# Weights loaded and split ahead of the first attention; experts chosen by the least 1+exp(-z); hot rows fetched at stage 3; the first maxima of layer F interleaved

## The chip, the cores and the metric

The kernel runs on one core of one Trainium2 chip. The time is the device time in microseconds (us) of one execution. Five engines work side by side, each on its own list of instructions, and wait for each other on semaphores: TensorE (PE, with its weight load as PEld), VectorE (DVE), ScalarE (ACT), GpSimd (POOL) and SyncE (SP), which issues most of the DMAs. TensorE runs at one of two clocks, 1.2 or 2.4 GHz; the profile gives the granted share (0.50 or 1.00).

## The reference, cut to what matters

Eight sequences (batches 0 to 7) of 512 tokens by 128 go through two layers.

```python
x = x + A(layernorm(x))      # A: z = layernorm(x); 16 heads of causal softmax(z_h k_h) v_h, k = z Wk + bk,
                             # then z + gelu(o + bv) @ Wf + bf
x = x + F(layernorm(x))      # F: 8 heads, 8 experts
# in F, per token and head:
gates = sigmoid(x @ w_gate)                 # 8 per head
sel = argmax(gates, axis=-1)
gm = one_hot(sel) * gates                   # only the chosen expert's gate is left
values = einsum(gm, value_experts, x)       # the values are those of the chosen expert, times its gate
out = softmax(q k / 8, causal) @ values
out = einsum(gm, output_experts, out)       # the chosen expert again, on the way out
```

All weights are the same for the eight batches.

## The kernel before

One batch after another goes through layer A's attention (`attention_a` on PE and DVE, `attention("A", b)` on ACT and POOL), the `turn` (gelu, projection back, layer norm of layer F), `experts` (gates, queries and keys, expert values) and layer F's attention, in which the work on batch b+1 (its normalised input, its keys, its first maxima) is already mixed. Every engine has its own program, written out by hand; the order in the code is the order on the engine, and a wait in it holds up all that is behind it on that engine.

**Precision.** Every weight and activation that PE multiplies is split in a high and a low half (`wq_h`, `wq_l`), so a projection is three matmuls (lines 426 to 428, `mm3`). The high half is a copy on ACT, the low half a subtraction on DVE. The weights of layer F (`wq`, `wkf`, `wg`: 0.5 MB; `ve`: 2 MB) are loaded by four DMAs at the end of the restacking of batch 0 (line 407), into space that `hots` and `oe_sb` use later, and split when ACT and DVE come to group 2 of batch 0's attention A (`expert_weights_high`, `expert_weights_low`, `SPLIT_AT`).

**Attention.** Heads go in 4 groups, each group in 3 stages (the causal triangle of 4 tiles of 128 keys: tile 0, tile 1, tiles 2 and 3). A *max unit* (PE scores into `ps_max`, DVE masks them and takes row minima, line 1096) and its *denominator* (ACT exp with sum, line 812) come first; 12 units a group in A, 6 in F. Then `negate` (DVE) forms the negative of maximum plus logarithm, PE transposes it, ACT copies it to `mt_a` or `mt_f`, and SP writes it by DMA as extra rows (`maxima_rows`, line 345, semaphore `mrow`) into the stacked queries, so that the second pass of scores (`ps_exp`) comes out normalised. ACT takes its exp (line 870), POOL cuts the triangle (line 992), PE weighs the values (line 589). Group g+2's max units are mixed into group g's scores; groups 0 and 1 need theirs ahead.

**Stacked operands.** Layer A's queries and keys are cut into three bf16 parts, written to DRAM (`parts_q`, `parts_k`, line 296) and read back in stacked rows (lines 303, 306, 314) into `s1q` and `s2k`, of which 96 rows are multiplied. Rows that carry nothing must hold zeros: before, DVE zeroes all of `s1q` (line 1334) and POOL all of `s2q` and `s2k` (lines 1006, 1007). Layer F's queries and keys go from `pt` to `s1q`, `s1k`, `s2q`, `s2k` by 12 DMAs for each pair of heads (`restack_f`, line 334, semaphores `pair_sent0` and `pair_sent1`), 48 for a batch; pairs 2 and 3 reuse the space of pairs 0 and 1 in `pt`.

**experts(f).** PE makes the gates (bank 4) and 8 projections `qk` (u = 0 to 7; even ones queries, odd ones keys). ACT copies the high half (line 919, `qk_hi`), DVE makes the low half (line 1269, `qk_lo`), and SP sends a pair as soon as its two low halves are there. After u = 3, 5 and 7 come 12, 10 and 10 of the 32 *expert values* (n = 0 to 31, token tile and expert): three matmuls into bank n % 4; the first expert of a tile is copied by ACT, the other seven are picked by DVE with a predicated copy (line 1296, 28 of them). The banks of `qk` before are u % 2. The picks need `hot`, the one-hot choice that `gate_ops` computes on DVE. Before, in 7 steps: g_w = 1 + exp(-z); its reciprocal (the gates, 256 columns, line 1219); their maximum over 8 experts; which equal it; times a rank, so that ties go to the first; the maximum of that; which equal it. `outputs_end(f-1)` (line 1156) adds the last batch's residual after u = 0, and SP stores it (line 373) in `store(b-1)`, which stands ahead of `restack_f` in SP's list. Layer F's first 12 max units are mixed into the values from n = 20 on, one for each n; ACT takes their denominators after all of `experts`, at the head of `attention("F", b)`.

**The way out.** `hots` (the chosen rows, 64 partitions by 8 KB twice, from `hot_d`) is fetched four times a batch by DMAs that ACT issues (line 791), at the stages in `HOTS_AT`; DVE multiplies with it (`choose`, line 1146) from unit 14 of layer F on.

## Time and profile before

| | us |
|---|---|
| median of 3 runs | 1428.21 |
| lowest and highest | 1423.2, 1431.45 |
| the profiled execution, whole | 1432.81 |
| its span, first to last instruction | 1430.8 |
| PE busy in the span | 1186.2 (83%) |
| DVE, ACT, POOL busy | 895.1, 903.9, 213.8 |
| mean granted TensorE clock | 0.934 |

The chain of work that ended last is spread over many lines; 14% of it is "issue", time in which an engine waited for nothing that the page names, the longest pieces of it 10.85 us at 52.58 us and 3 us at 99.21 us. Batches follow each other every 168 to 171 us. A timeline row gives start and length in us, engine, line, what is written and read, and in brackets the idle time of the engine before it and what ended it.

### The profile page before, as it was taken

The page shows a single profiled execution, that of the slowest core. Times are in us where ns is not written, and L with a number is a line of the kernel's source. Part 1 is how long each engine was busy: PE and PEld are TensorE (multiplying, and loading weights), DVE is VectorE, ACT ScalarE, POOL GpSimd, SP SyncE. Part 2 cuts the span into 40 slices and gives each one's busy share as a digit, 9 for nine tenths or more (in the row PEclk, how much of TensorE's full clock was granted, in tenths as well). Part 3 has the DMA queues.
Part 4 walks back from the last instruction along what each step waited for, and adds up shares of the span by engine and source line. Part 5 has one row for each costly group of instructions (what it writes and reads, how often), then busy time and mean ns, then how long its engine had stood idle before and what let it go on. Part 6 is the DMA issues. An engine that isn't in the chain of part 4 may idle for free.

```text
span 1430.8 us, 19696 instructions
## 1 busy us (share of the span) xinstructions
PE 1186.2 (83%) x5720; PEld 644.8 (45%) x5720; DVE 895.1 (63%) x2786; ACT 903.9 (63%) x2551; POOL 213.8 (15%) x264
## 2 busy tenths in 40 slices
PE   2567988888987889788897898878898789978888
PEld 1113753256532564236542474325653356424653
DVE  5552857648574676737676485755757477673855
ACT  1784387935778266962769447783677827696361
POOL 3011011201112011120111111120111211111010
PEclk9566999999999999999999999999999999999999
DMA  2401734126421453206432073313632155320723
GB/s 80 125 2 61 179 87 94 31 68 141 113 54 33 113 138 94 61 3 149 117 78 60 25 172 101 80 31 84 149 95 49 33 129 125 90 61 3 174 64 74
DMA packets 64177, 122.32 MB, mean 85 GB/s; under 512 B 14099, under 2 KB 29843, under 8 KB 59683
## 3 DMA queue, kind: packets, MB, share of 16 engines
q1 hardware_dynamic: 58950, 87.50, 24.5%
q10 hardware_dynamic: 5120, 33.56, 10.5%
q8 instruction: 46, 0.75, 0.2%
q14 instruction: 61, 0.50, 0.1%
HBM read 61.11 MB, written 9.06 MB: 49 GB/s over the span
## 4 chain that ended last, share of the span: by engine, by line
PE 42%; ACT 20%; DVE 19%; issue 14%; POOL 2%; DMA 1%; ACTq 0%; SPq 0%; DVEq 0%; POOLq 0%
ACT masked L812 9%; ACT pt L870 8%; PE ps_o L589 8%; PE ps_m L598 7%; DVE masked L1096 5%; PE ps_m L426 3%; PE ps_exp L506 3%; PE ps_exp L507 3%; PE ps_m L427 2%; PE ps_m L428 2%; PE ps_max L693 2%; PE ps_exp L508 2%; DVE val L1296 2%; PE ps_exp L426 2%; DVE at L1146 2%
## 5 line engine op out<-in xcount | busy, mean ns | idle before, releaser
L1096 DVE CUSTOM_DVE_ANT_0 masked<-ps_max,mask 128x512 f32<-128x512 f32 (+3 forms) x768 | 353.5, 487 | 210.5 <-PE ps_max L506 90.4
L812 ACT ACTIVATE masked<-masked,low 128x512 f32<-128x512 f32 (+3 forms) x768 | 427.0, 559 | 71.2 <-DVE low L1096 67.2
L870 ACT ACTIVATE pt<-ps_exp 128x384 f32<-128x384 f32 (+1 forms) x576 | 293.2, 523 | 125.7 <-PE ps_exp L508 69.9
L992 POOL TENSOR_SCALAR_AFFINE_SELECT pt<-pt 128x512 f32<-128x512 f32 (+2 forms) x192 | 137.1, 714 | 742.0 <-ACT pt L870 742.0
L598 PE MATMUL ps_m<-at,oe_sb 128*128 128x512 f32 x416 | 219.1, 616 | 5.7 <-DVE at L1146 3.5
L506 PE MATMUL ps_exp<-s1q,s2k 96*128 96x128 bf16 (+3 forms) x512 | 137.1, 325 | 96.5 <-ACT pt L870 83.0
L589 PE MATMUL ps_o<-pt,val 128*32 128x128 f32 (+6 forms) x1536 | 193.6, 481 | 9.1 <-POOL pt L992 9.1
L1146 DVE TENSOR_TENSOR at<-osb,hots 128x512 f32<-128x512 f32 x208 | 143.3, 690 | 32.2 <-PE ps_m L598 32.2
L506 PE MATMUL ps_max<-s2k,s1q 96*128 96x512 bf16 (+3 forms) x512 | 138.6, 320 | 20.1 <-DVE low L1096 11.9
L506 PEld LDWEIGHTS ps_exp<-s1q,s2k 96*128 96x128 bf16 x512 | 42.3, 100 | 248.3 <-ACT pt L870 197.6
L812 ACT ACTIVATION_READ_ACCUMULATOR masked<-masked,low 128x1 f32 x768 | 150.3, 196 | 0.0
L507 PE MATMUL ps_exp<-s1q,s1k 128*128 128x256 f32 (+2 forms) x256 | 100.8, 404 | 14.8 <-issue 11.6
L1296 DVE COPY_PREDICATED val<-osb,ps_exp 128x512 f32<-128x512 uint32 x128 | 92.0, 734 | 26.5 <-PE ps_exp L428 26.4
L589 PEld LDWEIGHTS ps_o<-pt,val 128*32 128x32 f32 (+1 forms) x1536 | 53.5, 122 | 90.2 <-issue 58.9
L506 PEld LDWEIGHTS ps_max<-s2k,s1q 96*128 96x128 bf16 x512 | 48.8, 100 | 95.1 <-DVE low L1096 46.4
L598 PEld LDWEIGHTS ps_m<-at,oe_sb 128*128 128x128 f32 x416 | 70.2, 192 | 39.0 <-DVE at L1146 27.6
L507 PE MATMUL ps_max<-s1k,s1q 128*128 128x256 f32 (+2 forms) x256 | 86.5, 347 | 1.3 <-DVE low L1096 1.3
L919 ACT ACTIVATE pt<-ps_m 128x512 fp32r<-128x512 f32 x64 | 38.3, 598 | 73.9 <-PE ps_m L428 72.3
L508 PE MATMUL ps_max<-s2k,s2q 96*128 96x256 f32 (+2 forms) x256 | 84.3, 339 | 0.0
L508 PE MATMUL ps_exp<-s2q,s2k 96*128 96x256 f32 (+2 forms) x256 | 84.0, 338 | 0.0
L1317 DVE TENSOR_TENSOR x<-ps_max,x 128x512 f32<-128x512 f32 x8 | 5.5, 692 | 124.4 <-PE ps_max L693 124.4
L507 PEld LDWEIGHTS ps_exp<-s1q,s1k 128*128 128x128 f32 x256 | 50.4, 197 | 69.3 <-issue 49.7
(156 smaller groups left out, 1750.1 us busy)
## 6 DMA issues: line engine op xcount, KB each, us to landing
hots<-hot_d ACTq DMA_DIRECT2D x64, 512.0 KB, 6.6
s1q<-pt SPq DMA_DIRECT2D x128, 128.0 KB, 2.3
s1k<-pt SPq DMA_DIRECT2D x128, 128.0 KB, 2.3
s1q<-parts_q SPq DMA_DIRECT2D x96, 96.0 KB
s2k<-parts_k SPq DMA_DIRECT2D x96, 96.0 KB
s2q<-pt SPq DMA_DIRECT2D x64, 128.0 KB, 2.3
s2k<-pt SPq DMA_DIRECT2D x64, 128.0 KB, 2.3
parts_q<-pt SPq DMA_DIRECT2D x24, 128.0 KB, 2.3
```

The costliest lines, as they stand in the source:

```text
L426: mm(dst, lh, rh, start=True, stop=False)
L506: return mm(dst, l1[0:KROWS, h, l2], r1[0:KROWS, h, r2], start=True, stop=True)
L507: mm(dst, l1[0][:, h, l2], r1[0][:, h, r2], start=True, stop=False)
L508: return mm(dst, l1[1][0:KROWS, h, l2], r1[1][0:KROWS, h, r2], start=False, stop=True)
L589: last = mm(ps_o[g % 2][j * w:j * w + w, qt * P:S], val[:, kt, h * w:h * w + w], pt[:, (n % 2) * 4 + j, c0:c1], start=kt == 0, stop=kt == 3)
L598: mm(ps_m[1][:], oe_sb[:, u], chosen_o(u), start=u == 0, stop=u == T * E - 1).then_inc(at_used.sem, 1)
L812: last = nc.scalar.activation(e, e, ACT.Exp, bias=low[:, g % 2, c:c + 1], scale=-1.0, accum_out=den[:, g % 2, c:c + 1])
L870: nc.scalar.activation(pt[:, (n % 2) * 4 + j, 0:c1 - c0], ps_exp[u % 2][:, c0:c1], ACT.Exp).then_inc(exp_done[k].sem, 1)
L992: nc.gpsimd.affine_select(out=v, in_=v, compare_op=ALU.is_ge, fill=0.0, base=0, pattern=[[0, HG[k]], [0, m], [1, P]], channel_multiplier=- ...
L1096: last = v.tensor_tensor_reduce(out=masked[:, u % JUNK, c0:c0 + w], in0=src[:, c0:c0 + w], in1=mask[:, S - w:S], scale=-1.0, scalar=POS, o ...
L1146: v.tensor_tensor(chosen_o(u), osb[:, u // E], hots[:, u // E % 2, u % E], ALU.mult).then_inc(at_done.sem, 1)
L1296: v.copy_predicated(val[:, t].rearrange("p (h k) -> p h k", k=64), pick, ps_m[BANK[("F", "moe1", n)]][:].rearrange("p (h k) -> p h k", k=6 ...
```

## The change

Five edits are made.

1. **Start, SP.** The four loads of layer F's weights stand behind the five loads of `x`, `ident`, `wk`, `wv`, `bk`, ahead of the constants. The memsets of `s1q`, `s2q`, `s2k` on DVE and POOL are gone; in their place three DMAs fill rows 64 to 95 of each with zeros (32 partitions by 16 KB each), behind a wait for the constants in DRAM. The rows of ones and the parts of k come behind a wait for these zeros.
2. **Start, ACT and DVE.** The weights are split ahead of attention A of batch 0, ACT's half behind `k_part1(0)`, DVE's behind `values_a(0)`.
3. **experts, DVE and PE.** The choice is made on g_w = 1 + exp(-z) itself: the minimum over the experts, which are at most that, rank, maximum, which equal. The reciprocal is taken of the 32 minima alone. The first two steps stand ahead of u = 0, the others between u = 0 and u = 2; `log_gates` follows u = 2 and `outputs_end(f-1)` u = 3. `qk` uses banks u % 4.
4. **experts, the first max units of layer F.** They stand at n = 13, 14, 16, 17, 19, 20, 22, 23, 25, 26, 28, 29, on PE, DVE and ACT alike: ACT takes the denominators there, no longer behind the loop. `negate` of group 0 moves from n = 27 to 23, its transpose from 30 to 25, and ACT copies `mt_f` at 27.
5. **HOTS_AT.** In layer F the first fetch of `hots` moves from stage 1 to stage 3 (of 12).

```diff
-BANK.update({("F", "qk", u): u % 2 for u in range(8)})
+BANK.update({("F", "qk", u): u % 4 for u in range(8)})
...
-MAX_FROM, NEGATE_AT, TRANSPOSE_AT = 20, 27, 30
+NEGATE_AT, TRANSPOSE_AT, COPY_AT = 23, 25, 27
+MAX_AT = {13 + 3 * m // 2: (m,) for m in range(N_MAX)}
...
-HOTS_AT = {("F", 1): 0, ("F", 9): 1, ("A", 0): 2, ("A", 4): 3}
+HOTS_AT = {("F", 3): 0, ("F", 9): 1, ("A", 0): 2, ("A", 4): 3}
...
+            for dst, src in ((raw["wq"], wq), (raw["wkf"], wkf), (raw["wg"], wg),
+                             (ve_raw, ve.rearrange("p (e n) -> p e n", n=S))):
+                sp.dma_start(dst, src).then_inc(w_in[2].sem, 16)
             sp.dma_start(zeros_d, consts[5:9]).then_inc(cst.sem, 16)
...
-            sp.wait_ge(cst.sem, cst.count(0, 16 * 3))
-            sp.wait_ge(set_p.sem, set_p.count(0, 3))
...
+            sp.wait_ge(cst.sem, cst.count(0, 16 * 3))
+            for dst in (s1q, s2q, s2k):
+                sp.dma_start(dst[64:96].bitcast(F32).rearrange("p h n -> p (h n)"), zeros_d[0].partition_broadcast(32)
+                             ).then_inc(zero_rows.sem, 16)
...
             parts_to_dram(0, "q")
+            sp.wait_ge(zero_rows.sem, zero_rows.count(0, 16 * 3))
+            sp.dma_start(ks[STACK:STACK + PARTS], onesb_d.rearrange("p (h n) -> p h n", n=S)).then_inc(cst.sem, 16)
             parts_to_dram(0, "k")
...
-            for dst, src in ((raw["wq"], wq), (raw["wkf"], wkf), (raw["wg"], wg),
-                             (ve_raw, ve.rearrange("p (e n) -> p e n", n=S))):
-                sp.dma_start(dst, src).then_inc(w_in[2].sem, 16)
...
-                    if g == SPLIT_AT and k == "A" and b == 0:
-                        expert_weights_high()
...
+                            for m in MAX_AT.get(n, ()):
+                                denominators("F", f, *divmod(m, STAGES * HG["F"]))
+                                if m == STAGES * HG["F"] - 1:
+                                    logs("F", f, 0)
+                            if n == COPY_AT:
+                                maxima("F", f, 0)
...
             k_part1(0)
+            expert_weights_high()
...
-            nc.gpsimd.memset(s2q[:].bitcast(F32), 0.0).then_inc(set_p.sem, 1)
-            nc.gpsimd.memset(s2k[:].bitcast(F32), 0.0).then_inc(set_p.sem, 1)
...
+                step(1, v.tensor_scalar(g_w, g_s, 1.0, None, ALU.add))
+                after(1)
+                step(2, v.tensor_reduce(wlow[:], by_head(g_w), AX.X, ALU.min))
+                yield
...
+                v.tensor_copy(hot_b, hot.rearrange("p (t c) -> p t c", c=64)).then_inc(gt_ready.sem, 1)
+                step(7, v.reciprocal(gmax[:], wlow[:]))
...
-                step(2, v.reciprocal(g_s, g_w))
...
-                    if u == 0 and f > 0:
+                    if u < 3:
+                        next(gates)
+                    if u == 2:
+                        log_gates(f)
+                    elif u == 3 and f > 0:
                         outputs_end(f - 1)
...
-            v.memset(s1q[:].bitcast(F32), 0.0).then_inc(set_v.sem, 1)
...
             values_a(0)
+            expert_weights_low()
```

SP's list at the start, before (the loads of `x`, `ident`, `wk`, `wv`, `bk` stand ahead of it):

```order
L281 DMA zeros_d<-in_consts 16x1024
L282 DMA ones_d<-in_consts 16x512
L283 DMA onesb_d<-in_consts 16x1536
L286 DMA s2k<-onesb_d 3x8192 [waits set_p,cst]
L287 DMA bf_sb<-in_bf 128x128
L288 DMA bv_sb<-in_bv 128x4
L289 DMA wf_sb<-in_wf 128x512
L296 DMA parts_q<-pt 16x8x512 [waits q1]
L296 DMA parts_q<-pt 16x8x512 [waits q2]
L296 DMA parts_q<-pt 16x8x512 [waits q3]
L296 DMA parts_k<-pt 16x8x512 [waits k1]
```

Now (the loads of `wq`, `wkf` and `wg` stand just ahead of this piece):

```order
L283 DMA oe_sb<-in_ve 128x4096
L284 DMA zeros_d<-in_consts 16x1024
L285 DMA ones_d<-in_consts 16x512
L286 DMA onesb_d<-in_consts 16x1536
L287 DMA bf_sb<-in_bf 128x128
L288 DMA bv_sb<-in_bv 128x4
L289 DMA wf_sb<-in_wf 128x512
L292 DMA s1q<-zeros_d 32x4096 [waits cst]
L292 DMA s2q<-zeros_d 32x4096
L292 DMA s2k<-zeros_d 32x4096
L300 DMA parts_q<-pt 16x8x512 [waits q1]
L300 DMA parts_q<-pt 16x8x512 [waits q2]
```

The four weight loads have moved ahead of the constants, the rows of ones (`s2k<-onesb_d`) to behind the last part of q, and three DMAs of zeros, each of 32 rows, stand between the constants and the parts.

DVE's list in `experts` of batch 1, around the low halves of u = 0, 1 and 2 (the rows that write to `pt`), before:

```order
L1269 SCALAR_TENSOR_TENSOR pt<-ps_m,pt 128x512 [waits qk_hi]
L1156 TENSOR_TENSOR at<-ps_max,x_0 128x512 [waits out_ready]
L1214 TENSOR_REDUCE zmax<-ps_max 128x32 [waits gate_ready,gate_exp]
L1216 TENSOR_SCALAR osb<-osb 128x256
L1219 RECIPROCAL osb<-osb 128x256 [waits gate_step]
L1246 TENSOR_SCALAR zlow<-zmax 128x32 [waits gate_exp]
L1248 SCALAR_TENSOR_TENSOR zabs<-zlow,zmax 128x32 [waits low_gate]
L1269 SCALAR_TENSOR_TENSOR pt<-ps_m,pt 128x512 [waits qk_hi]
L1222 TENSOR_REDUCE gmax<-osb 128x32 [waits gate_step]
L1225 TENSOR_TENSOR osb<-osb,gmax 128x256 [waits gate_step]
L1269 SCALAR_TENSOR_TENSOR pt<-ps_m,pt 128x512 [waits qk_hi]
L1229 TENSOR_TENSOR osb<-osb,rank 128x256 [waits gate_step]
```

Now:

```order
L1220 TENSOR_SCALAR osb<-osb 128x256 [waits gate_exp]
L1222 TENSOR_REDUCE wlow<-osb 128x32 [waits gate_step]
L1272 SCALAR_TENSOR_TENSOR pt<-ps_m,pt 128x512 [waits qk_hi]
L1225 TENSOR_TENSOR osb<-osb,wlow 128x256 [waits gate_step]
L1228 TENSOR_TENSOR osb<-osb,rank 128x256 [waits gate_step]
L1272 SCALAR_TENSOR_TENSOR pt<-ps_m,pt 128x512 [waits qk_hi]
L1232 TENSOR_REDUCE wmax<-osb 128x32 [waits gate_step]
L1234 TENSOR_TENSOR osb<-osb,wmax 128x256 [waits gate_step]
L1272 SCALAR_TENSOR_TENSOR pt<-ps_exp,pt 128x512 [waits qk_hi]
L1238 CAST osb<-osb 128x256 [waits gate_step]
L1239 RECIPROCAL gmax<-wlow 128x32
L1245 TENSOR_REDUCE zmax<-ps_max 128x32 [waits gate_ready]
```

The long reciprocal (`osb<-osb 128x256`) is gone, a short one of 32 columns stands behind the choice, and the residual (`at<-ps_max,x_0`) has moved from the second row to behind the low half of u = 3, four rows below the last that is shown.

ACT's list in `experts` of batch 1, behind the copies for u = 4 and 5, before:

```order
L745 ACTIVATE val<-ps_m 128x512 [waits moe1_ready] x2
L919 ACTIVATE pt<-ps_m 128x512 [waits pair_sent1,qk_ready]
L919 ACTIVATE pt<-ps_m 128x512 [waits qk_ready]
L812 ACTIVATE masked,den<-masked,low 128x512 [waits max_doneF]
L812 ACTIVATE masked,den<-masked,low 128x256 [waits max_doneF]
L812 ACTIVATE masked,den<-masked,low 128x128
L812 ACTIVATE masked,den<-masked,low 128x384 [waits max_doneF]
```

Now:

```order
L816 ACTIVATE masked,den<-masked,low 128x512 [waits max_doneF]
L816 ACTIVATE masked,den<-masked,low 128x256 [waits max_doneF]
L816 ACTIVATE masked,den<-masked,low 128x128
L749 ACTIVATE val<-ps_m 128x512 [waits moe1_ready]
L816 ACTIVATE masked,den<-masked,low 128x384 [waits max_doneF]
L749 ACTIVATE val<-ps_m 128x512 [waits moe1_ready]
L816 ACTIVATE masked,den<-masked,low 128x512 [waits max_doneF]
L816 ACTIVATE masked,den<-masked,low 128x256 [waits max_doneF]
L816 ACTIVATE masked,den<-masked,low 128x128
L816 ACTIVATE masked,den<-masked,low 128x384 [waits max_doneF]
L831 ACTIVATE lnd<-den 128x8 [waits neg_stepA,den_doneF]
```

Denominators (`masked,den`) now stand between and behind the copies of values for tiles 2 and 3 (`val<-ps_m`), ahead of the high halves of u = 6 and 7.

## Rows read from the trace of the kernel before

**Rows 1.** Timeline of DVE and POOL at the start.
```profile
2.16 3.47 DVE L1334 MEMSET s1q<- 128x4096 f32 x1 [0.80 <-issue]
...
8.05 7.53 DVE L1040 TENSOR_SCALAR xnA<-x_sb,mv,rstd 128x128 f32<-128x128 f32 x4 [1.20 <-POOL rstd L974]
...
7.96 3.51 POOL L1006 MEMSET s2q<- 128x4096 f32 x1
```
**Rows 2.** Timeline of SP and PE at the start (SP: issue times of DMAs).
```profile
22.04 2.63 SPq L296 DMA_DIRECT2D parts_k<-pt  x3
26.43 2.34 SPq L303 DMA_DIRECT2D s1q<-parts_q  x3
...
35.05 0.91 PE L506 MATMUL ps_max<-s2k,s1q 96*128 96x512 bf16 x3 [7.34 <-DMA s2k<-parts_k]
```
**Rows 3.** DMA issues of the whole run: count, KB each, median us to landing.
```profile
hots<-hot_d ACTq DMA_DIRECT2D x64, 512.0 KB, 6.6
...
oe_sb<-in_ve SPq DMA_DIRECT2D x1, 2048.0 KB, 18.5
```
**Rows 4.** Timeline of PE and ACT in attention A of batch 0.
```profile
63.43 0.59 PE L506 MATMUL ps_exp<-s1q,s2k 96*128 96x512 bf16 x1 [10.85 <-issue]
...
64.05 0.60 ACT L870 ACTIVATE pt<-ps_exp 128x512 f32<-128x512 f32 x1 [9.19 <-PE ps_exp L506]
...
98.37 0.61 PE L506 MATMUL ps_exp<-s1q,s2k 96*128 96x512 bf16 x1 [5.66 <-ACT pt L870]
```
**Rows 5.** Timeline of POOL, stages 5 and 11 of attention A, batches 0 and 2.
```profile
92.34 1.10 POOL L992 TENSOR_SCALAR_AFFINE_SELECT pt<-pt 128x1024 f32<-128x1024 f32 x1 [3.89 <-ACT pt L870]
...
121.21 1.10 POOL L992 TENSOR_SCALAR_AFFINE_SELECT pt<-pt 128x1024 f32<-128x1024 f32 x1 [3.15 <-ACT pt L870]
...
442.14 1.10 POOL L992 TENSOR_SCALAR_AFFINE_SELECT pt<-pt 128x1024 f32<-128x1024 f32 x1 [3.71 <-ACT pt L870]
...
460.92 1.10 POOL L992 TENSOR_SCALAR_AFFINE_SELECT pt<-pt 128x1024 f32<-128x1024 f32 x1 [1.95 <-ACT pt L870]
```
**Rows 6.** Windows: busy us (instructions) of PE, PEld, DVE, ACT, POOL; granted clock, DMA share, GB/s.
```profile
96.00:100.00 4.00, 0.90 (x2) 0.21 (x2) 2.13 (x1) 3.97 (x7) 0.00 (x0) 0.51 0.00 0
...
109.00:112.00 3.00, 2.86 (x13) 0.41 (x12) 0.00 (x0) 1.34 (x3) 1.10 (x1) 0.50 1.01 431
...
482.00:486.00 4.00, 3.73 (x9) 2.26 (x10) 3.61 (x9) 1.20 (x2) 0.00 (x0) 0.60 0.57 133
...
490.00:494.00 4.00, 4.00 (x21) 2.94 (x20) 3.96 (x14) 0.34 (x1) 1.01 (x1) 1.00 0.87 202
```
**Rows 7.** Timeline of DVE in `experts` of batch 2.
```profile
477.72 0.69 DVE L1269 SCALAR_TENSOR_TENSOR pt<-ps_m,pt 128x512 fp32r<-128x512 f32 x1 [3.06 <-ACT pt L919]
...
479.57 1.75 DVE L1219 RECIPROCAL osb<-osb 128x256 f32<-128x256 f32 x1
...
487.01 1.43 DVE L1296 COPY_PREDICATED val<-osb,ps_exp 128x512 f32<-128x512 uint32 x2 [1.10 <-PE ps_exp L428]
...
495.87 1.28 DVE L1269 SCALAR_TENSOR_TENSOR pt<-ps_m,pt 128x512 fp32r<-128x512 f32 x2
```
**Rows 8.** Timeline of SP in `experts` of batch 2: first send, first row of maxima.
```profile
482.21 1.17 SPq L334 DMA_DIRECT2D s1q<-pt  x2
...
516.57 1.44 SPq L345 DMA_DIRECT2D s2q<-mt_f  x2
```
**Rows 9.** Timeline of PE and ACT where layer F's attention begins, batch 2.
```profile
519.21 0.47 PE L507 MATMUL ps_exp<-s1q,s1k 128*128 128x512 f32 x1 [0.52 <-issue]
...
523.33 0.47 PE L426 MATMUL ps_m<-xh,wk_h 128*128 128x512 f32 x1 [2.00 <-DVE xl L1045]
...
521.68 0.60 ACT L870 ACTIVATE pt<-ps_exp 128x512 f32<-128x512 f32 x1
```
**Rows 10.** Timeline of PE and DVE, batch 2: group 1's scores, first use of `hots`.
```profile
532.73 0.55 PE L507 MATMUL ps_exp<-s1q,s1k 128*128 128x512 f32 x1 [2.04 <-issue]
...
546.64 0.69 DVE L1146 TENSOR_TENSOR at<-osb,hots 128x512 f32<-128x512 f32 x1
```

More of the change, by code:

```diff
@@ L67 @@
 VALUES_AT = {p: range(*r) for p, r in enumerate(((0, 0), (0, 12), (12, 22), (22, T * E)))}
-MAX_FROM, NEGATE_AT, TRANSPOSE_AT = 20, 27, 30
+NEGATE_AT, TRANSPOSE_AT, COPY_AT = 23, 25, 27
 N_MAX = 2 * STAGES * HG["F"]
-MAX_AT = {MAX_FROM + n: range(N_MAX * n // (T * E - MAX_FROM), N_MAX * (n + 1) // (T * E - MAX_FROM))
-          for n in range(T * E - MAX_FROM)}
+MAX_AT = {13 + 3 * m // 2: (m,) for m in range(N_MAX)}
 def choices(n):
@@ L996, in gated_values @@
             def gated_values(f):
+                pool.wait_ge(gate_step.sem, gate_step.count(f, GS))
                 for t in range(T):
@@ L1172, in attention_a @@
                 for g in range(GROUPS):
-                    if g == SPLIT_AT and a == 0:
-                        expert_weights_low()
                     for s in range(STAGES):
```

62 lines of the change are left out of this document (25 added, 37 removed).

## The prediction

> **What bounds the kernel now.** I read the timelines of the start first, then the waits and timelines of one batch (the third, batch 2), then windows for the clock and for what DMA moves.
>
> The start is a line of waits. DVE zeroes `s1q`, and its four normalisations take 7.53 us, since each of the long ones ends with one of POOL's two memsets of 3.51 us beside it [rows 1]. The parts of k are sent at 22.0, the restacking begins at 26.4 and PE's first scores at 35.1 [rows 2]. Later PE waits 10.85 us for the first row of maxima, ACT 9.19 us; that row stands behind the 2 MB of `ve`, which takes 18.5 us to land [rows 3, 4]. At group 2 ACT and DVE split the weights and PE waits 5.66 us [rows 4]; its clock falls to half and stays there [rows 6]. Stages 5 to 11 of attention A take 28.87 us in batch 0 and 18.78 in batch 2, which also has the last batch's products in them [rows 5].
>
> In `experts` DVE is busy nearly all along, but SP's list is as long: from the first send to the first row of maxima 34.36 us pass [rows 8]. I count 48 sends at 0.64 us each (two issues of one pair take 1.17 in the row [rows 8], later ones 1.24), some 31 us. So two things set where layer F's attention begins: DVE's picks and SP's issues. In layer F's stages, PE then waits at group 1 for a row of maxima (2.04 us in batch 2) that shares the DMA engines with 1 MB of `hots` [rows 3, 10].
>
> **The change part by part.** The sum is made against the profiled execution, 1432.81 us whole, which lies 4.6 above the median of the runs, 1428.21.
>
> *The start.* Without the memsets, `x` is there about 1.8 us before 5.55, where DVE took it up behind its memset (2.16 + 3.47 us), and the normalisations take about 1.1 us as in later batches: q and k are ready 8.2 us earlier [rows 1]. But SP can't send them. Its list now has 2.65 MB of weights, then the constants, a wait for these, and 1.57 MB of zeros. The nearest rows for the rate are a load to 128 partitions, 431 GB/s, and the sends to 64 partitions, 202 GB/s [rows 6]. Weights at 431 from 5.7 us on (when the first loads are in): 6.1 us, and some 2.5 us for constants and landing: SP goes on at 14.5. The zeros go to 32 partitions, so I take the row with the fewer partitions: 1.57/202 is 7.8 us, from 16 to 24. Then the parts of k, 2.2 us to land, and the restacking begins at 28.3 where it was 26.4: **2 us lost**. Bounds: both at 431, 1.8 us gained; both at 202, 8.7 lost. The splits themselves (4.7 us on ACT, 6 on DVE) start at about 14 and 20 and are over before the first scores; if the weights landed after 24 they would add what they come late.
>
> The Trainium skill, "SBUF — State Buffer", section "Door 1: The DMA port swizzle", says that the bandwidth of a DMA hangs on how many of 16 ports its partitions reach, and that partitions 64 to 95 reach 8, no fewer than 64 partitions do. By that rule the zeros run at the rate of the sends, and the 202 I took stands; by the 431 of the full load the start would gain 4 us over my figure. The two rates in the rows differ by about 2, as the rule has it.
>
> *Attention A of batch 0.* The first row of maxima has no 2 MB ahead of it, so ACT goes on from its last denominator and not 9.19 us later [rows 4]: **9.1 gained**. At worst the row lands 2 us late by itself, 7 gained. The split is gone from group 2. With PE not idle there I expect it to keep the full clock, so stages 5 to 11 go as in batch 2, less DVE's and PE's products: 28.87 less 18 [rows 5]: **11 gained**. If the clock stays at half, six stages take 3.75 us each as stages 9 to 11 did, 22.5, and 6.4 are gained.
>
> *experts, the choice.* From the first low half to the last step before the picks DVE now takes 477.72 to 485.91, which is 8.2 us, and then waits 1.10 for PE [rows 7]. Out go the reciprocal's 1.75 less about 0.27 for 32 columns, two steps (0.7) that now stand in the 3.06 us of idle time ahead of u = 0, and a wait of 0.2. That leaves 5.8: the picks start at 483.6 and not 487.01, since with four banks PE doesn't wait for low halves. By that alone **3.4 us** would be gained a batch.
>
> *What gives most of it back.* The residual moves from behind u = 0, where it ended at 479.0, to behind u = 3, at about 483.6. SP's store waits for it, and behind the store stand all 48 sends. So the first send goes from 482.21 to 484.15 [rows 8], **1.9 us later**, though its data is there 2 us earlier. Then SP issues without a break: 48 by 0.64, one for `hot_d` and about 0.8 for single slow issues, 32.3 us in all: the row of maxima goes out at about 516.0 instead of 516.57, 0.6 us gained. ACT waits for pair 0's sends ahead of u = 4, to 494.1, so the low halves there start at 494.2 and not 495.87 [rows 7]; the picks and 12 max units behind take 22 us in either order, and end at about 517, ahead of SP.
>
> *What the denominators' new place brings.* Before, ACT came to the next batch's input at 520.7, behind the last two denominators that stood behind DVE's last max unit, and to its first exp at 521.68 [rows 9]. Now these are done earlier; it waits for pair 3's sends (517.8) and PE's first scores (518.7, where it was 519.21, and 0.87 to their end). First exp at 519.6: 2.1 us earlier. The keys, for which PE waited 2.00 us at 523.33 [rows 9], come at 520.8, 2.5 earlier. I take **2.3 us** a batch. Bounds: 0.6, if only SP counts, and 3.4, if a stalled send costs less than I think.
>
> *hots at stage 3.* The wait at group 1 is 2.04 us in batch 2 [rows 10], 0 to 2.2 in the eight batches and about 1 on average; the row of maxima then has only the parts of q beside it: **0.9** a batch. The 1 MB now runs beside the restacking, which nothing needs for some 8 us. The first product is at 546.64, the fetch at about 529: with 6.6 us to land there are 11 us of room [rows 3, 10]. Bounds: -0.5 to 1.2.
>
> *Sum.* Start -2, attention A of batch 0 9.1 + 11, batch 0's experts 4 (no store stands in SP's way there, so most of the 3.4 and the ACT part arrive), batches 1 to 6 six times 3.2, batch 7 1.5 (no next batch to prepare): 42.8 us. 1432.8 - 42.8 is 1390.0 by the profiled execution and 1385.4 by the median; I say **1388**.
>
> **The rivals.**
>
> *SP alone decides* (22%). The row of maxima goes out 0.6 us earlier and ACT and PE find nothing to do with the rest; for it speaks that SP's list has no slack left, against it that the next batch's input and keys don't hang on that row. Batches 1 to 7 give 0.6 + 0.4 each: 2 us short of the forecast each. 1388 + 15 is 1403; with a slow issue a batch 1407.
>
> *The start costs more* (12%). Zeros and weights at 202 GB/s and the half clock kept in attention A: 6.7 + 4.6 us: 1399.
>
> *More comes through* (14%). Zeros at 431, 3.4 us a batch: 4 + 7: 1377.
>
> *Nothing comes of it* (5%): the two above together, and a slow landing of the zeros, some 13 us more: 1420 to 1430.
>
> *Slower than before, by the clock* (4%). PE is idle 2.81 us ahead of u = 3 before, and the window shows a granted 0.60 for it [rows 6]. Now PE waits some 3 us ahead of u = 4's low half instead, with 20 values and 12 max units behind. At half clock three matmuls take 1.28 us and not 0.70, so each us at half clock costs 0.46. Before, it came back within 3 us; in batch 0 it stayed down for 24 us behind the 10.85 us of idle time. If it stays down for T us in each batch, the loss is 0.46 T less the 1.7 us by which the picks are ahead of SP. From T = 16 on this eats 5.6 us a batch, all that is gained; at 20, 7.5 by 8 is 60 us: 1448. The short break speaks against it.
>
> **How the numbers follow.** The forecast has 43%, own range 1380 to 1396. The range 1372 to 1410 takes in the first three rivals and their bounds and leaves out the last two, and part of the tails. A measurement of this kernel can tell about 0.5%, 7 us, from no change: faster 0.93, same 0.03, slower 0.04.
>
> **What would show it.** Right: DVE's four `xnA` in about 1.1 us; first scores at 35 to 39; no wait over 2 us at the first `ps_exp` of batch 0; windows of attention A's stages 5 to 11 at full clock; picks of batch 2's kind starting 5.9 us after the first low half; SP's first send right behind the store, and no gap between its 48 sends; keys within 2.5 us of the first scores. Wrong: a first send that isn't later, since then the picks' 3.4 come through; a wait of DVE for `hots`; zeros that land after 30 us; a granted clock under 0.9 in the second half of `experts`.

## The result and the profile after

The changed kernel takes 1450.4 us in the median (four runs, 1440.5 to 1452.6) and the kernel before 1425.9 on the same chip (four, 1423.2 to 1431.5): the ratio is 1.0153, 95% interval 1.0094 to 1.0212. It is **slower by 1.5%**; the prediction had 1388, and 4% for slower. The profiled execution has a span of 1450.2 us, that of the kernel before 1430.8.

**The start** went much as forecast. Timelines of DVE, SP and PE of the changed kernel; the columns are start, duration, engine, line, operation, and in brackets the idle time before and what ended it:

```profile
6.46 1.11 DVE L1049 TENSOR_SCALAR xnA<-x_sb,mv,rstd 128x128 f32<-128x128 f32 x4 [1.20 <-POOL rstd L984]
...
14.47 0.34 SPq L292 DMA_DIRECT2D s1q<-zeros_d  x1
...
24.24 0.29 SPq L404 DMA_DIRECT2D s2k<-onesb_d  x1
...
28.18 2.35 SPq L307 DMA_DIRECT2D s1q<-parts_q  x3
...
37.64 0.91 PE L509 MATMUL ps_max<-s2k,s1q 96*128 96x512 bf16 x3 [17.00 <-DMA s2k<-parts_k]
...
56.18 0.58 PE L509 MATMUL ps_exp<-s1q,s2k 96*128 96x512 bf16 x1 [0.82 <-issue]
```

The normalisations take 1.11 us, SP goes on at 14.5, the zeros are in at 24.2, and the first scores stand at 37.64, 2.6 us later than before [rows 2]. PE's wait of 10.85 us ahead of the first `ps_exp` [rows 4] is now 0.82. Windows of attention A of batch 0 and of the zeros' transfer (busy time by engine, granted clock, DMA share, GB/s), then POOL's timeline at the ends of stages 5 and 11:

```profile
60.00:76.00 16.00, 12.91 (x71) 3.98 (x70) 9.63 (x44) 15.62 (x52) 2.74 (x4) 0.95 0.01 2
76.00:112.00 36.00, 31.52 (x152) 8.50 (x151) 5.30 (x25) 27.30 (x70) 7.08 (x9) 0.50 0.17 61
...
20.00:24.00 4.00, 0.64 (x2) 0.00 (x0) 3.41 (x6) 0.00 (x0) 0.00 (x0) 1.00 0.89 195
```

```profile
85.57 1.10 POOL L1002 TENSOR_SCALAR_AFFINE_SELECT pt<-pt 128x1024 f32<-128x1024 f32 x1 [4.17 <-ACT pt L873]
...
108.41 1.10 POOL L1002 TENSOR_SCALAR_AFFINE_SELECT pt<-pt 128x1024 f32<-128x1024 f32 x1 [3.15 <-ACT pt L873]
```

From 76 to 112 us the clock is at its lower level although PE has no wait of 0.8 us or more there; from the end of stage 5 to that of stage 11 it is 22.84 us.

**experts** of batch 2, SP, DVE and PE:

```profile
478.36 0.68 DVE L1165 TENSOR_TENSOR at<-ps_max,x 128x512 f32<-128x512 f32 x1
478.95 1.34 DVE L1298 COPY_PREDICATED val<-osb,ps_exp 128x512 f32<-128x512 uint32 x2
...
479.06 0.40 SPq L377 DMA_DIRECT2D out<-at  x1
479.51 1.17 SPq L338 DMA_DIRECT2D s1q<-pt  x2
...
511.87 0.60 SPq L338 DMA_DIRECT2D s2k<-pt  x1
512.77 1.43 SPq L349 DMA_DIRECT2D s2q<-mt_f  x2
...
509.05 0.28 PE L550 MATMUL ps_m<-ident_sb,nm_f 128*16 128x128 f32 x1 [0.86 <-DVE val L1298]
...
512.80 0.50 PE L429 MATMUL ps_m<-ve_h,xh 128*128 128x512 f32 x1 [1.25 <-ACT mt_f L749]
...
516.53 0.60 PE L446 MATMUL ps_m<-ident_sb,xnA 128*128 128x128 f32 x4
516.98 0.47 PE L510 MATMUL ps_exp<-s1q,s1k 128*128 128x512 f32 x1
```

The picks begin 15.0 us behind the batch's turn (DVE's last addition of layer A, at 463.98 in batch 2); before it was 18.5 [rows 7]. But the first send stands behind the store, the row of maxima goes out right behind the last send, and PE, which waited 0.52 us ahead of its first scores [rows 9], doesn't wait at all: it is itself late. It waited 0.86 and 1.25 us for PSUM bank 0, which the transposition of the maxima borrows in the middle of the values: first the transposition waits until DVE has picked from the bank, then value 28 waits until ACT has copied the maxima out of it.

In the kernel before, the row of maxima did not stand right behind the sends. SP's last send ended at 515.31, and the row went out at 516.57 [rows 8], as soon as ACT had copied it (first SP, then ACT):

```profile
514.71 0.60 SPq L334 DMA_DIRECT2D s2k<-pt  x1
...
516.27 0.27 ACT L745 ACTIVATE mt_f<-ps_m 16x128 f32<-16x128 f32 x1 [0.68 <-PE ps_m L547]
```

So what held the row there was not the end of SP's list but the values and maxima ahead of ACT's copy. They stand behind `u` = 4, whose high half ACT makes only when pair 0's sends have landed; in the changed kernel ACT waits 2.59 us for them, until 488.99. That is how a late first send reaches all that follows.

**Layer F** of batch 2, PE, then SP and ACT's queue:

```profile
541.11 0.80 PE L510 MATMUL ps_exp<-s1q,s1k 128*128 128x512 f32 x1 [5.04 <-DMA s2q<-mt_f]
...
525.30 2.24 SPq L300 DMA_DIRECT2D parts_k<-pt  x3
...
532.05 1.58 SPq L318 DMA_DIRECT2D s2k<-parts_k  x3
533.67 1.44 SPq L349 DMA_DIRECT2D s2q<-mt_f  x2
...
526.97 0.62 ACTq L795 DMA_DIRECT2D hots<-hot_d  x1
```

The wait for group 1's row [rows 10] is gone, and one of 5.04 us stands at group 2. In the groups of the page the scores of layer F wait 33.2 us in all, 32.9 of it for such a row (3.9 to 5.5 us in each of batches 0 to 6):

```profile
L510 PE MATMUL ps_exp<-s1q,s1k 128*128 128x256 f32 (+2 forms) x256 | 103.7, 416 | 33.2 <-DMA s2q<-mt_f 32.9
```

The wait also costs clock. Windows ahead of the scores at 541.11 and behind them, in the changed kernel; in the kernel before, the clock is 1.00 in all of 537 to 549 us:

```profile
537.00:541.00 4.00, 0.00 (x0) 0.00 (x0) 0.00 (x0) 0.00 (x0) 0.00 (x0) 0.71 0.39 118
541.00:545.00 4.00, 3.90 (x13) 2.09 (x15) 1.33 (x7) 2.50 (x6) 0.42 (x1) 0.50 0.17 66
```

The same marks in all traces, worked out from their timelines. "First turn" is absolute; first send, row of maxima out, first scores are us behind the turn, "rest" runs from the first scores to the next turn, all means of batches 1 to 6. The ratio is to the kernel before, with its 95% interval:

| kernel | median | ratio | first turn | send | row out | scores | rest |
|---|---|---|---|---|---|---|---|
| before | 1425.9 | 1 | 127.9 | 13.7 | 49.0 | 51.6 | 117.6 |
| changed | 1450.4 | 1.015 (1.009, 1.021) | 117.1 | 15.5 | 49.7 | 53.8 | 119.7 |
| e8 before, new start | 1419.9 | 0.990 (0.984, 0.996) | 114.2 | 13.7 | 48.9 | 51.6 | 116.8 |
| e4 hots 1, old order | 1419.7 | 0.990 (0.984, 0.995) | 116.0 | 15.5 | 48.9 | 51.6 | 117.8 |
| e1 hots 1 | 1426.2 | 0.995 (0.991, 0.998) | 114.9 | 15.5 | 49.5 | 53.6 | 117.0 |
| e2 old order | 1447.6 | 1.010 (1.007, 1.014) | 115.4 | 15.5 | 49.3 | 52.0 | 121.6 |
| e3 residual early | 1421.9 | 0.992 (0.988, 0.995) | 114.7 | 11.9 | 45.9 | 50.1 | 118.5 |
| e14 store behind pair 1 | 1414.6 | 0.990 (0.985, 0.995) | 114.5 | 11.3 | 45.4 | 49.5 | 118.7 |
| e10 = e3, row first | 1409.7 | 0.987 (0.983, 0.991) | 116.0 | 11.9 | 45.9 | 50.1 | 117.6 |
| e7 before, hots 3 | 1471.6 | 1.027 (1.021, 1.033) | 130.1 | 13.7 | 49.2 | 51.9 | 122.7 |
| e6 = e1 + e3 | 1402.3 | 0.977 (0.972, 0.983) | 114.9 | 11.9 | 46.0 | 50.1 | 117.3 |
| e9 = e6, row late | 1423.2 | 0.992 (0.987, 0.996) | 116.9 | 11.9 | 48.2 | 50.9 | 118.6 |
| e12 = e9, store late | 1420.5 | 0.994 (0.991, 0.998) | 114.7 | 11.3 | 48.7 | 51.4 | 117.1 |
| e5 = e6, old order | 1394.8 | 0.973 (0.968, 0.978) | 117.2 | 11.9 | 45.7 | 48.4 | 117.1 |
| e11 = e5, store late | 1400.1 | 0.981 (0.977, 0.985) | 113.6 | 11.3 | 46.5 | 49.1 | 118.1 |
| e15 = e5, row first | 1391.9 | 0.973 (0.967, 0.978) | 116.7 | 11.9 | 45.7 | 48.3 | 116.6 |
| e13 = e5, hots 0 | 1386.9 | 0.971 (0.965, 0.977) | 115.5 | 11.9 | 45.7 | 48.3 | 115.5 |
| e16 = e13, row first | 1380.1 | 0.966 (0.961, 0.971) | 114.1 | 11.9 | 45.7 | 48.3 | 116.1 |

The kernel before had medians of 1426 to 1435 us in the different sets of runs, so sets are compared by their ratios.

### The profile page after: what moved, and what is told of

It reads as the page before. It is cut to its first block, busy times and chain, and to the rows that moved or that the text cites. A ratio compares the mean times of both kernels' runs of the same rounds, so it can differ in the third digit from the quotient of the medians.

```text
span 1450.2 us, 19695 instructions
## 1 busy us (share of the span) xinstructions
PE 1193.9 (82%) x5720; PEld 651.8 (45%) x5720; DVE 878.2 (61%) x2785; ACT 902.3 (62%) x2551; POOL 205.0 (14%) x262
## 3 DMA queue, kind: packets, MB, share of 16 engines
q1 hardware_dynamic: 59094, 89.08, 24.2%
## 4 chain that ended last, share of the span: by engine, by line
PE 36%; ACT 20%; DVE 17%; issue 11%; DMA 8%; SPq 5%; POOL 2%; ACTq 0%; DVEq 0%; POOLq 0%
ACT masked L816 10%; PE ps_m L601 7%; PE ps_o L592 7%; ACT pt L873 7%; DVE masked L1105 4%; SPq L338 3%; PE ps_exp L509 3%; DMA s2q<-mt_f 3%; DMA parts_k<-pt 3%; PE ps_exp L510 2%; PE ps_max L696 2%; DVE val L1298 2%; DVE pt L1272 2%; PE ps_exp L511 2%; DVE at L1155 2%
## 5 line engine op out<-in xcount | busy, mean ns | idle before, releaser
L592 PE MATMUL ps_o<-pt,val 128*32 128x128 f32 (+6 forms) x1536 | 197.9, 493 | 7.8 <-POOL pt L1002 7.8
L509 PE MATMUL ps_max<-s2k,s1q 96*128 96x512 bf16 (+3 forms) x512 | 143.6, 330 | 29.9 <-DMA s2k<-parts_k 17.0
L510 PE MATMUL ps_exp<-s1q,s1k 128*128 128x256 f32 (+2 forms) x256 | 103.7, 416 | 33.2 <-DMA s2q<-mt_f 32.9
L509 PEld LDWEIGHTS ps_max<-s2k,s1q 96*128 96x128 bf16 x512 | 50.1, 103 | 109.0 <-issue 57.6
L429 PE MATMUL ps_m<-ve_h,xh 128*128 128x512 f32 x128 | 55.4, 433 | 36.7 <-DVE pt L1272 26.7
L510 PE MATMUL ps_max<-s1k,s1q 128*128 128x256 f32 (+2 forms) x256 | 83.4, 336 | 0.0
```

The source lines that it names most:

```text
L429: mm(dst, lh, rh, start=True, stop=False)
L509: return mm(dst, l1[0:KROWS, h, l2], r1[0:KROWS, h, r2], start=True, stop=True)
L510: mm(dst, l1[0][:, h, l2], r1[0][:, h, r2], start=True, stop=False)
L592: last = mm(ps_o[g % 2][j * w:j * w + w, qt * P:S], val[:, kt, h * w:h * w + w], pt[:, (n % 2) * 4 + j, c0:c1], start=kt == 0, stop=kt == 3)
```

## The experiments

**Which edit costs.** Four kernels, one edit undone or done alone. The first puts the fetch of `hots` back:

```diff
-HOTS_AT = {("F", 3): 0, ("F", 9): 1, ("A", 0): 2, ("A", 4): 3}
+HOTS_AT = {("F", 1): 0, ("F", 9): 1, ("A", 0): 2, ("A", 4): 3}
```

> The changed kernel with the first fetch of hots back at stage 1 of layer F, the rest of the change kept. In the trace of the changed kernel PE waits 3.9 to 5.5 us at group 2 of layer F in batches 0 to 6 for a row of maxima that was issued 2.4 us before it was needed and took 7.4 us to land; before, the wait stood at group 1 and was 0 to 2.2 us. Theory H (the fetch at stage 3 holds up the parts of k, the restacking behind them and the row of group 2): that wait goes, about 2 us come back at group 1, 3 us a batch are saved, seven batches, about 1429 us against 1450. Rival R (the wait is the restacking's own doing, since the parts and their restacking now come earlier in the batch than before): the wait of group 2 stays with the fetch at stage 1, and the time stays within 5 us of 1450.

1426.2 us, 24 less than the changed kernel, 29 by the ratios: theory H. The long wait is gone (0.37 us in one batch of seven) and 1.83 us are back at group 1; "rest" falls from 119.7 to 117.0. The same number in the kernel before:

```diff
-HOTS_AT = {("F", 1): 0, ...
+HOTS_AT = {("F", 3): 0, ...
```

> The kernel before with one number changed: the first fetch of hots at stage 3 and not stage 1. Theory H: 3 us a batch are lost as in the changed kernel, seven times, about 1426 + 21 = 1447, with a wait of 4 to 5 us at group 2. Rival R (the collision comes only with the earlier end of experts): within 5 us of 1426. The prediction had this edit at 0.9 us a batch gained: 1420.

1471.6 us, ratio 1.027: worse than theory H had it, 5.1 us a batch and not 3. Where nothing else changes, the fetch at stage 3 costs some 38 us by the ratio (30 to 47 by its interval); in batch 2:

```profile
545.72 0.45 ACTq L791 DMA_DIRECT2D hots<-hot_d  x1
...
542.03 4.74 SPq L296 DMA_DIRECT2D parts_k<-pt  x3
...
552.88 1.44 SPq L345 DMA_DIRECT2D s2q<-mt_f  x2
...
560.76 0.80 PE L507 MATMUL ps_exp<-s1q,s1k 128*128 128x512 f32 x1 [5.57 <-DMA s2q<-mt_f]
```

The waits at group 2 are 4.2 to 5.7 us, and about 1.3 us of waits at groups 1 and 2 go with them (0.4 to 2.2 in the kernel before), so they don't make up the 5.1 us alone. Behind the wait the granted clock is 0.50 in 560 to 564 us and 0.85 in 564 to 568, and something like it follows in every batch.

Next the residual back behind `u` = 0:

```diff
+                    if u == 0 and f > 0:
+                        outputs_end(f - 1)
                     if u < 3:
                         next(gates)
                     if u == 2:
                         log_gates(f)
-                    elif u == 3 and f > 0:
-                        outputs_end(f - 1)
```

> The changed kernel with the residual (and so SP's store) behind the low half of u = 0 as before, all else as changed. The first send moves from 15.5 to about 13.7 us behind the turn. Theory S (SP's list decides): 1.8 us a batch are saved in batches 1 to 7, about 12 us, 1438. Theory O (DVE with PE and ACT decides): the row of maxima doesn't move, the time stays within 4 us of 1450, or rises by up to 0.7 a batch, since the residual's 0.7 us now stands ahead of the choice: 1455.

1421.9 us, 34 less than the changed kernel by the ratios and more than theory S had: the first send and the row of maxima move by 3.6 and 3.7 us. The send now waits only for the low half of `u` = 1 (462.26 and 0.69 us, the send at 462.97 in batch 2), and the shorter steps of the choice have moved that up by 1.8 us against the kernel before.

And the order of the maxima as before, with the denominators and logarithms back in ACT's layer F:

```diff
-NEGATE_AT, TRANSPOSE_AT, COPY_AT = 23, 25, 27
+MAX_FROM, NEGATE_AT, TRANSPOSE_AT = 20, 27, 30
-MAX_AT = {13 + 3 * m // 2: (m,) for m in range(N_MAX)}
+MAX_AT = {MAX_FROM + n: range(N_MAX * n // (T * E - MAX_FROM), N_MAX * (n + 1) // (T * E - MAX_FROM))
+          for n in range(T * E - MAX_FROM)}
```

> The changed kernel with the order of layer F's first maxima as before (twelve units behind value 20 and on, the denominators and logs in layer F, the row of maxima transposed behind value 30), hots left at stage 3. In the changed kernel the stretch from the low half of u = 4 to the last pick of batch 2 takes 27.8 us where it took 24.0, with DVE waiting for PE and ACT between the picks. Theory O (spreading the units among the values makes DVE, ACT and PE wait for each other): the stretch goes back to 24 us, the picks end 3.5 us earlier, of which ACT gives 1.2 back since the denominators return to layer F; 2 us a batch, some 16 us, about 1434. Rival S (SP's 48 sends set the row of maxima whatever DVE does): first scores stay at 48 to 51 us behind the turn, and the time goes up by the 1.2 a batch, about 1458.

1447.6 us against 1450.4 in another set (ratios 1.010 and 1.015), no difference to speak of, neither theory. First scores come 1.8 us earlier, "rest" is 1.9 longer, which I put down to the denominators, now in layer F again (no run has them alone), and PE still waits 4.3 to 5.4 us for the row of group 2.

**Do they add, and what is the rest worth?**

> The changed kernel with both: the first fetch of hots at stage 1 and the residual behind u = 0. If the two losses stand in different places (hots in layer F's stages, the store ahead of the sends in experts) they add: from the traces of the two kernels that had one each, the first scores come 50.1 us behind the turn and the next turn 117.4 us later, 167.5 a batch; 115 + 7 x 167.5 + 115 is 1402 us. Rival (they trade with each other, as an earlier row meets the fetch again): 1415 to 1422, no better than the residual alone.

Both together (e1 and e3): 1402.3 us, as the sum had it. The losses stand in different places.

> As the kernel with hots at stage 1 and the residual behind u = 0, and also the order of layer F's first maxima as before. Now SP's sends begin 3.6 us earlier, so what the order of the maxima is worth can be seen where SP doesn't hide it. Theory (spread units are worth something once SP is out of the way): the row of maxima waits for DVE's units at 48 us behind the turn, first scores at 51 and the keys 1.2 us later: 2 us a batch worse than 1402, 1416 us. Rival (the order is worth nothing or costs): 1402 or less.

1394.8 us (1392.9 to 1395.9, e6 1399.8 to 1407.6): the rival. With SP out of the way the old order is not worse but 7.5 us better than the spread one. PE at the beginning of layer F, first of e6, then of e5:

```profile
495.22 0.28 PE L550 MATMUL ps_m<-ident_sb,nm_f 128*16 128x128 f32 x1 [0.86 <-DVE val L1298]
498.98 0.50 PE L429 MATMUL ps_m<-ve_h,xh 128*128 128x512 f32 x1 [1.25 <-ACT mt_f L749]
502.70 0.60 PE L446 MATMUL ps_m<-ident_sb,xnA 128*128 128x128 f32 x4
```

```profile
497.05 0.27 PE L551 MATMUL ps_m<-ident_sb,nm_f 128*16 128x128 f32 x1
498.89 0.60 PE L447 MATMUL ps_m<-ident_sb,xnA 128*128 128x128 f32 x4
500.30 0.47 PE L511 MATMUL ps_exp<-s1q,s1k 128*128 128x512 f32 x1 [0.80 <-issue]
```

The row goes out at nearly the same time in both (46.0 and 45.7 us behind the turn); in e6 PE comes to its scores 1.7 us later, in e5 it waits for the row.

> The changed kernel with hots at stage 1 and the old order of the maxima: of the change only the start, the choice by least 1+exp(-z) with its four banks and the residual behind u = 3 are left. Theory S (SP's list decides when layer F begins, so earlier picks give nothing): first scores at 52 us behind the turn as before, all that is left is the start's 12 us: 1416 to 1420. Rival D (DVE's picks decide, as the prediction had it for half): 3.4 us a batch more, some 1394.

> The kernel before with the new start alone (weights ahead of zeros, zeros by DMA, the split behind the first values). The prediction had 18 us for it; the trace of the changed kernel has the first turn 10.8 us earlier, three kernels with the same start 12.5 to 13.2. Expected: 1426 - 12 = 1414 to 1418. With the start's 18 us: 1408.

1419.7 and 1419.9 us, both with ratio 0.990. So of the change the start alone gives 1%, and the choice, with its residual behind `u` = 3, **nothing**, though its picks begin 4.4 us earlier (15.0 behind the turn, 19.4 without it). The same choice with the residual behind `u` = 0 (e5) gives 25 us more, 3.6 a batch, about what the prediction had for the choice by itself (3.4). No run parts the choice from its four banks.

How the late store takes these 25 us shows in the marks of e4 and e5. The row goes out 3.2 us later in e4, each time within 0.1 us of ACT's copy, and in four batches of six 1.3 us or more behind the last send. The low half of `u` = 4 comes 1.7 us later (25.9 and 24.3 us behind the turn, means), since pair 0's sends land later. PE waits 3.3 to 4.5 us there and not 1.4, and the clock falls behind that wait. So from the low half of `u` = 4 to that of `u` = 6 it takes 11.9 us and not 10.3, the other 1.5. Windows of e4 behind its wait, then of e5:

```profile
480.00:484.00 4.00, 4.00 (x11) 3.17 (x12) 2.17 (x5) 0.00 (x0) 0.00 (x0) 0.57 0.89 207
```

```profile
478.00:482.00 4.00, 4.00 (x19) 3.23 (x18) 2.77 (x4) 1.16 (x2) 1.08 (x2) 1.00 0.79 183
```

**Is it SP's list or DVE's?** The changed kernel with only the store moved in SP's list, behind the 24 sends of pairs 0 and 1:

```diff
                 for p in range(4):
+                    if p == 2 and f > 0:
+                        store(f - 1)
                     if p == 2:
                         hots_to_dram(f)
...
-                if b > 0:
-                    store(b - 1)
                 layer_f(b)
```

> The changed kernel with one line of SP's list moved: the store, whose data is there behind u = 3, is issued behind the 24 sends of pairs 0 and 1 and not ahead of them. DVE's list is untouched, the residual stays behind u = 3, hots stay at stage 3, the maxima stay spread. Theory S (the sends wait for the store, nothing else of the residual's place costs): first send at 11.3 us behind the turn instead of 15.5, as much or more comes back as with the residual behind u = 0 (28 us): 1416 to 1424. Rival D (the residual behind u = 3 costs on DVE): 1440 to 1450.

1414.6 us, 36 less than the changed kernel (2.5% by the ratios too), a little under what theory S had. DVE's list is the same, the residual is where the change put it. SP in batch 2 of it:

```profile
468.09 1.17 SPq L340 DMA_DIRECT2D s1q<-pt  x2
...
483.51 0.59 SPq L379 DMA_DIRECT2D out<-at  x1
...
502.04 1.43 SPq L351 DMA_DIRECT2D s2q<-mt_f  x2
```

First send at 11.3 us behind the turn and the row out at 45.3: the place of the *store*, not that of the residual, decided.

**The spread order and its bank.** e6 with the row of maxima made later:

```diff
-NEGATE_AT, TRANSPOSE_AT, COPY_AT = 23, 25, 27
+NEGATE_AT, TRANSPOSE_AT, COPY_AT = 27, 30, 30
```

> The kernel with hots at stage 1 and the residual behind u = 0 (1402 us), units still spread from value 13, but the row of maxima made later: negated behind value 27, transposed behind 30, copied behind 30. In the changed kernel's trace PE waits 0.86 us for a pick ahead of that transposition, which borrows bank 0 of the values behind value 25, and 1.25 us for ACT's copy ahead of value 28, which wants the bank back. Theory B (the borrowed bank is what the spread order costs): both waits go, first scores at 48.4 us behind the turn instead of 50.0, keys at 51.2, about 1390. Rival W (DVE's and ACT's waits between the spread picks cost, wherever the row is made): PE's first scores stay at 50, and the row itself goes out later than 46 behind the turn: 1402 to 1410.

1423.2 us, ratio 0.992 (e6 0.977): neither theory, and 13 us over rival W's range. The two waits of theory B go, and the last pick ends 48.6 us behind the turn and not 50.6, so the borrowed bank did cost 2 us. But ACT comes to the copy only behind its denominators, so the row goes out at 48.2 and not 46.0, and PE waits for it:

```profile
505.37 0.66 PE L446 MATMUL ps_m<-ident_sb,xnA 128*128 128x128 f32 x4 [1.04 <-ACT mt_f L749]
507.98 0.77 PE L510 MATMUL ps_exp<-s1q,s1k 128*128 128x512 f32 x1 [1.95 <-issue]
```

The clock falls behind these waits as well: it is 0.70 in 506 to 510 us and 0.50 in 510 to 514, where e6 has 1.00 at the same place, and "rest" is 1.3 us longer. So the bank is what PE waits for in e6, but the one later place that was tried costs more; whether another is free, no run shows.

Then e5 with SP's store behind the sends of pair 0:

```diff
-                    if u == 0 and f > 0:
+                    if u == 1 and f > 0:
                         outputs_end(f - 1)
...
+                    if p == 1 and f > 0:
+                        store(f - 1)
```

> The kernel with hots at stage 1, the old order of the maxima and the residual behind u = 0 (1394.8 us); now the residual stands behind u = 1 and SP's store behind the 12 sends of pair 0, so no send waits for the residual. First send at 11.3 us behind the turn, not 11.9. If SP's list decides: 0.6 us and the store's issue a batch, some 4 to 7 us: 1389. If DVE's picks and maxima decide now: within 3 us of 1394.8.

1400.1 us, ratio 0.981 (0.977, 0.985), and with the spread order

> Both of the last two on one kernel: hots at stage 1, units spread from value 13 with the row made late, residual behind u = 1, store behind pair 0's sends. If both give what their theories say, they add: about 1384. If the spread units cost in themselves (rival W), about 1400.

1420.5 us, ratio 0.994. By the ratios these are no better than e5 and e9. Sends that begin 0.6 us earlier give nothing: in half of the batches of e11 the row goes out at 45.7 as in e5, in the others at 47.2. The difference is the clock. In the late batches (1, 3 and 4; in e12 1 and 6) it is at its lower level for some 3 us from about 15 us behind the turn, and `u` = 4's low half comes at 25.8 and not 24.3. Windows of e11 at this place in batch 1, then in batch 2:

```profile
294.00:298.00 4.00, 3.88 (x10) 3.12 (x11) 2.17 (x4) 0.00 (x0) 0.00 (x0) 0.57 0.87 203
463.50:467.50 4.00, 3.91 (x17) 3.20 (x18) 3.59 (x7) 0.00 (x0) 0.00 (x0) 1.00 0.88 204
```

PE's waits ahead of it are the same in both (0.9 and 0.8 us), so why the clock fell in one and not in the other stays open.

**How the fetch delays a row of 4 KB.** e3 (hots at stage 3) with the row of group 2 issued ahead of the restacking of k, and not behind:

```diff
                     restack_q(g)
+                    if g < 2:
+                        maxima_rows("F", f, 2 + g)
                     if g == 0:
                         sp.wait_ge(parts_out["k"].sem, ...)
                     restack_k(g)
-                    if g < 2:
-                        maxima_rows("F", f, 2 + g)
```

> The kernel with hots at stage 3 and the residual behind u = 0 (1421.9 us), and SP issues the row of maxima of group 2 ahead of the wait for the parts of k and of their restacking, not behind them. Theory Q (with hots at stage 3 this row is late because it stands in SP's queue behind 288 KB of restacking, which in turn wait for parts of k slowed by hots): the wait of 4 to 5 us at group 2 falls to 1 or less, 3 us a batch, about 1401. Rival M (the 1 MB of hots slows any transfer of this time, the row's too): the wait shrinks by the 1.3 us of the earlier issue or not at all, 1413 to 1422.

1409.7 us, between the two. The row is issued 1.2 to 2.0 us earlier, and the wait is 2.4 to 3.3 us and not 4.0 to 5.0; from issue to PE's scores it still takes 6.2 us:

```profile
519.10 1.43 SPq L349 DMA_DIRECT2D s2q<-mt_f  x2
...
525.30 0.50 PE L510 MATMUL ps_exp<-s1q,s1k 128*128 128x512 f32 x1 [2.66 <-DMA s2q<-mt_f]
```

Last, e5 with the fetch at the first stage:

```diff
-HOTS_AT = {("F", 1): 0, ...
+HOTS_AT = {("F", 0): 0, ...
```

> The kernel with the new start and choice, the residual behind u = 0, the old order of the maxima, and the first fetch of hots at stage 0 of layer F (1394.8 us with stage 1). At stage 0 the DMA engines have nothing else to do: the windows around the first scores show 0 to 70 GB/s. Theory (what costs is that the fetch runs beside the parts, the restacking and the rows): the 1.6 to 2.1 us of wait for group 1's row go, 1 us a batch, 1387. Rival (the fetch is in nobody's way at stage 1 but for chance): within 3 us of 1394.8.

1386.9 us, as forecast, "rest" 115.5 and not 117.1. The fetch goes out at 492.98, right with the first scores (491.66), where the DMA engines do next to nothing (9 GB/s in 489 to 493 us). The waits at group 1 are gone and 0.5 to 1.1 us stand at group 2.

> The kernel of 1394.8 us with the row of maxima of group 2 issued ahead of the wait for the parts of k (as tried with hots at stage 3, where the row was issued 1.2 to 1.9 us earlier and the wait shrank by 1.3 to 2.3). With hots at stage 1 that row is no more late in most batches (0.6 us in one), so nothing is to be had: within 3 us of 1394.8; if the restacking of k comes later by it and somebody waits for that, up to 5 us more.

1391.9 us, no difference, and both on one kernel

> Both of the last two: hots at stage 0 and the row of group 2 first. 1387 if stage 0 gives its 1 us a batch and the row nothing.

1380.1 us, ratio 0.966 (0.961, 0.971): 7 us better than forecast, though its trace has nothing for it in the marks but a start 1.4 us earlier. The waits at group 2 that e13 still has are gone too (none of 0.3 us or more in batches 0 to 6), but "rest" is no shorter, so I take the two as equal or nearly so. This is the fastest version, well ahead of both kernels: new start, least choice with four banks, residual and store behind `u` = 0, old order of the maxima, `hots` at stage 0.

## Why the prediction was wrong, point by point

- **The start: right in the parts, wrong in one.** Lost ahead of the first scores: 2.6 us (2 said). First exponentials 7.25 us earlier (9.1 less 2 said). The 11 us for stages 5 to 11 were 6.0 (28.87 to 22.84): the step "with PE not idle there I expect it to keep the full clock" failed, and the text's other branch, 6.4, held. The turn behind it, begun at half clock too, took 2 us more, so the first turn came 10.8 us earlier and not 18; e8 gives 1.0% in all, some 14 us.
- **The picks: right.** 5.8 us behind the first low half (5.9 said), and the choice is worth 3.6 us a batch where the residual stays behind `u` = 0 (e5 against e8).
- **The first send 1.9 us later: right** (1.8), **and not made good: wrong.** The prediction had the sends in 32.3 us, so that the row would go out 0.6 us earlier. They took 33.3 in batch 2 (479.51 to 512.77), and the row was 0.7 us later. The prediction's own terms give even less than it said: 484.15 and 32.3 us make 516.45, which is 0.1 us gained and not 0.6. Each term was within 1 us, but their difference had the wrong sign, and the only thing that paid for it was a shortening of a list that nothing in the change shortened. It also took the row as the end of SP's list, where it had waited 1.26 us more for ACT's copy; what the first send sets is when `u` = 4 can begin. "SP alone decides", given 22%, comes nearest to what experts did; its price too had this sign wrong, and its path is not the whole one.
- **The maxima "in either order": wrong.** The low half of `u` = 4 came as forecast, 25.6 us behind the turn (494.2 less 468.50 is 25.7). But from there to the last pick or max unit it took 27.8 us and not 22 nor the 24.0 of before, so the picks ended 53.5 us behind the turn and not 48.5 (517 said). That they ended at 517.5 in absolute time is no hit, since this batch's turn is 4.5 us earlier here. In the 27.8 are the 1.6 us of the lower clock behind the wait for `u` = 4, and 2.1 us by which the row of maxima in bank 0 held PE up. The scores came 4.2 us behind the row and not 2.7.
- **Input and keys: right in direction as a distance, lost in the sum.** The first exponentials stand 1.24 us behind the first scores (2.47 before), the keys 2.89 (4.12 before): 1.2 us each (the prediction had 0.9 and 2.1 us). But the scores came 2.2 us later (51.6 to 53.8).
- **hots at stage 3: wrong, and the largest error.** 0.9 us gained was said; it was 2.9 lost a batch in the changed kernel and 5.1 in the kernel before, 20 to 40 us in all, part of it by the lower clock behind the wait. The step that failed is "the 1 MB now runs beside the restacking, which nothing needs for some 8 us". That holds for the restacking; but the row of group 2 is issued behind it on the same queue, and PE needs it 2.4 us after its issue. I had looked at the row that moved out of the collision and not at what moved into it.
- **The clock rival: the step came, the price didn't.** PE stood idle ahead of `u` = 4 as it said (0.99 us busy in 486 to 490), the clock was 0.61 in the next 4 us and 0.96 in the 4 behind. That is 3 to 7 us at half clock in a batch, about what the kernel before had ahead of its picks, and far from the 16 us that the rival needed. Its 24 us for batch 0 are misread: in the kernel before the clock was at half already in 52 to 56 us, ahead of PE's 10.85 us of idle time and through it, and back by 80 us. The slower result came by SP's list and `hots`, neither of which was the rival that ended slower.
- **The first and the last batch: wrong.** Batch 0 had 4 us gained and took 3.0 more from turn to turn, batch 7 had 1.5 gained and took 1.5 more. Both have the spread order, and batch 0 the wait at group 2 (4.8 us).

By the two profiled executions: up to the first turn 10.8 us less (18.1 said), batch 0 3.0 more, batches 1 to 6 4.3 more each (3.2 less said), batch 7 1.5 more: 19.4 us more in all.

By the ratios, from before to changed: the start -1.0%, the choice with its late store 0 (without it 1.7 gained), the spread order +0.5, `hots` at stage 3 +2.1.

The Trainium skill, "DMA: Bandwidth & Descriptors", section "Queues, rings and completion order", says that the queues of SP and ACT share the same 16 DMA engines, and that each such engine adds its share to a transfer's semaphore only after all its own earlier writes, whatever queue they are from. The trace agrees as far as it goes: the parts of k, issued within 2.3 us of ACT's fetch, are waited for until 532.05, 4.5 us behind their last issue (median 2.3 on the page). Whether the order of completion or the shared rate does it, no run here tells apart. Of the zeros, the 195 GB/s of the window agree with the rule on ports that the prediction cited: they are near the 202 of the sends and under half of the 431.
